# In a four-layer conditional kernel, TensorE computes batch 1's first gate and up ahead of batch 0's first down product

## The reference

```
def _gemma_mlp(x, gate_w, up_w, down_w):
    g = jnp.einsum('bsh,hi->bsi', x, gate_w)
    u = jnp.einsum('bsh,hi->bsi', x, up_w)
    return jnp.einsum('bsi,ih->bsh', jax.nn.gelu(g, approximate=True) * u, down_w)
...
rw = softmax(cond_8);  w, sel = top_k(rw, 2);  w = w / w.sum()
out = sum over the two chosen e of  w[e] * _gemma_mlp(x, skill_gate[e], skill_up[e], skill_down[e])
out = out + _gemma_mlp(x, shared_gate, shared_up, shared_down)
x = x + out
...
up = x @ W_up[best].T + b_up ;  gate = x @ W_gate[best].T + b_gate
x = x + (silu(up) * gate) @ W_down[best].T + b_down
```

## Time and profile before

| | |
|---|---|
| median of 3 runs | 84.12 us (83.91 to 84.49) |
| time of the profiled execution | 85.01 us |
| its span | 83.7 us |
| around the span | 1.3 us |
| TensorE busy | 79.8 us, 95% |
| VectorE, ScalarE, GpSimd busy | 54.7, 37.8, 30.9 us |
| moved by DMA | 20.08 MB, mean 240 GB/s |

### The profile page before, as it was taken

How to read it: one execution, slowest core, us unless ns; L and a number is a source line. 1 busy time by engine, 2 the same in 40 slices (tenths; PEclk the granted TensorE clock), 3 DMA queues, 4 the chain that set the end, 5 groups by cost and what they waited for, 6 DMA issues and landing times.

```text
span 83.7 us, 1689 instructions
## 1 busy us (share of the span) xinstructions
PE 79.8 (95%) x560; PEld 73.8 (88%) x560; DVE 54.7 (65%) x121; ACT 37.8 (45%) x71; POOL 30.9 (37%) x32
## 2 busy tenths in 40 slices
PE   6999999999999999999979999999999999999960
PEld 6968998888888999999978998998998999999960
DVE  1468879865699851489953973973973973844360
ACT  6410895877555930727305434434432132162440
POOL 3020099297666992292900920830830000000000
PEclk9999999999999999999999999999999999999999
DMA  1998000599999998699868999999999954500102
GB/s 17 319 340 350 4 0 0 100 382 343 392 388 395 424 413 327 139 332 357 148 257 263 269 345 344 309 321 398 271 382 375 364 162 78 190 0 0 31 0 67
DMA packets 8792, 20.08 MB, mean 240 GB/s; under 512 B 976, under 2 KB 5200, under 8 KB 8784
## 3 DMA queue, kind: packets, MB, share of 16 engines
q1 hardware_dynamic: 8496, 19.20, 67.5%
q10 hardware_dynamic: 288, 0.79, 2.5%
HBM read 17.88 MB, written 0.52 MB: 220 GB/s over the span
## 4 chain that ended last, share of the span: by engine, by line
PE 86%; DMA 5%; SPq 2%; DVE 2%; issue 0%; DVEq 0%
PE bank L807 17%; PE bank L834 16%; PE bank L848 7%; DMA p<-p 5%; PE bank L863 4%; PE bank L770 4%; PE bank L778 4%; PE bank L786 4%; PE bank L709 4%; PE bank L701 3%; PE bank L820 3%; PE bank L817 3%; PE bank L818 3%; SPq L238 2%; PE bank L794 2%; PE bank L796 2%
## 5 line engine op out<-in xcount | busy, mean ns | idle before, releaser
L353 ACT ACTIVATE gelu<-bank 128x512 f32<-128x512 f32 x24 | 14.2, 595 | 24.0 <-PE bank L820 14.9
L317 POOL TENSOR_TENSOR wide_l<-first_w,wide_h 128x512 fp32r<-128x512 f32 x12 | 15.1, 1277 | 16.8 <-ACT wide_h L378 16.8
L569 DVE SCALAR_TENSOR_TENSOR hid<-gelu,wsel,bank 128x512 f32<-128x512 f32 x16 | 12.0, 747 | 13.1 <-PE bank L820 7.4
L807 PE MATMUL bank<-x_t,second_w 128*128 128x128 f32 x128 | 15.6, 275 | 0.0
L807 PEld LDWEIGHTS bank<-x_t,second_w 128*128 128x128 f32 x128 | 14.9, 192 | 0.0
L308 POOL TENSOR_TENSOR hid_l<-hid,hid_h 128x512 fp32r<-128x512 f32 x8 | 10.2, 1284 | 4.4 <-ACT hid_h L392 4.4
L848 PEld LDWEIGHTS bank<-x_t,w 128*128 128x128 f32 x64 | 8.2, 192 | 0.4
L834 PE MATMUL bank<-hid,second_w 128*128 128x128 f32 x64 | 8.5, 275 | 0.0
L848 PE MATMUL bank<-x_t,w 128*128 128x128 f32 x64 | 8.4, 275 | 0.0
L834 PEld LDWEIGHTS bank<-hid,second_w 128*128 128x128 f32 x64 | 7.9, 192 | 0.1
L567 DVE TENSOR_TENSOR hid<-gelu,bank 128x512 f32<-128x512 f32 x8 | 5.5, 687 | 2.9 <-ACT gelu L353 1.3
(11 more groups left out here) (85 smaller groups left out, 130.3 us busy)
## 6 DMA issues: line engine op xcount, KB each, us to landing
first_w<-in_skill SPq DMA_DIRECT2D x8, 768.0 KB, 6.1
second_w<-in_skill SPq DMA_DIRECT2D x8, 768.0 KB, 6.4
w<-in_layer SPq DMA_DIRECT2D x8, 384.0 KB, 6.5
p<-p SPq DMA_DIRECT2D x24, 64.0 KB, 4.1
rest_sb<-in_rest SPq DMA_DIRECT2D x1, 661.0 KB, 4.4
x_t<-in_x SPq DMA_DIRECT2D x1, 512.0 KB, 5.5
shared_sb<-in_shared ACTq DMA_DIRECT2D x1, 512.0 KB, 5.4
out_x<-out_sb SPq DMA_DIRECT2D x8, 64.0 KB, 4.0
```

The lines of the kernel that those rows point to most:

```text
L317: pool.tensor_tensor(wide_l[:, b % 2, m, :], w[:, m, :], wide_h[:, b % 2, m, :].bitcast(fp32), ALU.subtract).then_inc(wide_low, 1)
L353: act.activation(gelu[:, n, :], ps[:, :], ACT.Gelu_apprx_tanh).then_inc(gelu_ready, 1)
L569: dve.scalar_tensor_tensor(hid[:, n, :], gelu[:, n, :], wsel[:, bass.DynSlice(weight, 1)], u_ps[n][:, :], ALU.mult, ALU.mult).then_inc(hid ...
L807: mm = pe.matmul(ps[:, S * t:S * (t + 1)], w[:, 1 + n, 128 * t:128 * (t + 1)], x2_t[:, columns(b)], start=True, stop=True)
```

## The change

Two calls in TensorE's order change places. No wait, slot, buffer or other engine's order is changed.

```
@@ -907,8 +907,8 @@
                 shared_down(NSH - 3)
                 shared_down(NSH - 2)
                 shared_down(NSH - 1)
+                first_gate_up(1)
                 down(0, 0)
-                first_gate_up(1)
                 batch(1, 1, before_last=False)
```

## The result

The changed kernel takes 86.17 us (median of 4, 85.98 to 87.89) against 84.31 for the kernel before (4 runs). The ratio is 1.023, interval 1.017 to 1.029. The prediction's range ended at 85.1.

A forecast was written before the change was run, and what follows sets the result against it. TensorE was taken as the bound (86% of the chain), with batch 1's swap almost level at `down(1, 0)`. Parts 1 and 2 give 0, part 3 costs 0 to 0.3 us: 84.1 to 84.4, said 84.2, range 83.6 to 85.1.

The forecast's parts named there:

- Part 1: Batch 1's gate and up on TensorE start 0.90 us earlier, hidden values and transpose too; cost 0.
- Part 2: Batch 1's swap on SP, queued behind batch 3's second-expert load, is issued only 0.16 us earlier of 0.90.
- Part 3: `down(0, 0)` ends 1.38 us later, delaying batch 4's first-expert load ahead of the swap; cost 0 to 0.3 us.
- My own sum for the other engines: DMA engines other than the deciding one finish batch 1's swap at 41.9 to 42.4, still ahead of 42.61.
- Rival 1: At `down(1, 0)`: the DMA queue shifts as a whole, swap lands up to 1.38 us later, 85.5; chance 0.15.
- the straggler: DMA engine on the opening backlog until 36.6 sets the swap's landing as before, at 42.6 to 42.9.
- Rivals 2 and 3: At `down(1, 0)`: 2, wait of 0.44 us goes, 83.7, chance 0.15; 3, no wait before or after, 84.1, within 0.58.
- The last sentence of the sum: TensorE is the chain from 42.7 to 76 us, so nothing later gives back a change at `down(1, 0)`.

The follow-up runs named there:

- The kernel with the own tile: Changed order, batch 1's hidden values in a tile of their own so VectorE needn't wait for `down(0, 0)`: 1.018 of before, 85.70 us.
- changed order with five slots: Changed order plus a fifth slot for first experts, so batch 4's first load waits for nothing: 0.998 of before, 84.06 us.
- own tile with the load behind: Changed order, batch 1's hidden values in their own tile and batch 4's first-expert load behind batch 1's swap: 0.993 of before, 84.09 us.
- the run for theory C: Changed order, with the load of batch 4's second expert put behind the swap of batch 2: 1.029 of before, 86.53 us.
- the late-load kernel: Order of before, with batch 4's first-expert load held until batch 1's gate and up are done: 1.017 of before.
- the one with the load behind the swap: Changed order, with batch 4's first-expert load issued behind batch 1's swap: 0.993 of before, 84.17 us.
- the kernel with batch 1's swap first: Old order, with batch 1's swap issued ahead of batch 3's second-expert and batch 4's first-expert loads: 1.015 of before, 85.81 us.
- half the delay: Old order, with batch 4's first-expert load held until batch 1's gate is done: 1.013 of before, 85.57 us.
- The fifth slot: Old order plus a fifth slot for first experts, so batch 4's first load waits for nothing: 1.002 of before, 84.45 us.

## Why the prediction was wrong

**Part 1** failed in its second half. That gate and up could start at once was right: all six products run without a gap. But the hidden values were not made 0.90 us earlier. For batch 1's first expert VectorE waits at L565 for `down(0, 0)`, because that product reads the buffer about to be overwritten (batch 0 isn't in `TURNED`, so the exception in L564 doesn't apply). I read the rows of before, where this wait was always met, and not the code's condition. The new order puts that product last, and the transpose stayed where it was. The kernel with the own tile shows that this cost no time that the runs can tell (1.018 against 1.023).

**Part 2** was right for its own reason (SyncE stands behind `down(0, 1)`). The 0.16 us did not come either; the swap went out 0.59 us behind the second load where it was 0.54.

**Part 3, what the late load does to the landing, is the step that failed.** I argued that one DMA engine sets the landing, that it is on the opening backlog until 36.6, and that a later issue can't show on it; that such an engine ends its backlog before it begins the next load was my assumption, and no run shows it. From the issues and the flights of the L229 and L238 rows: the opening load landed at 36.6 before and 35.9 after, so the backlog was no later, and yet batch 4's load landed at 39.2 in place of 38.5, the next at 41.2 in place of 40.7, the last piece at 43.6 in place of 42.6. Windows of the changed kernel (DMA share and GB/s are the last two numbers), beside the earlier trace rows:

```profile
34.50:35.00 0.50, 0.50 (x7) 0.50 (x7) 0.48 (x1) 0.00 (x0) 0.50 (x1) 1.00 0.00 0
35.00:35.50 0.50, 0.50 (x7) 0.50 (x6) 0.47 (x2) 0.00 (x0) 0.50 (x2) 1.00 0.05 12
...
36.50:37.00 0.50, 0.50 (x6) 0.50 (x6) 0.28 (x2) 0.29 (x1) 0.04 (x1) 1.00 1.01 418
41.00:41.50 0.50, 0.50 (x7) 0.50 (x6) 0.48 (x2) 0.50 (x2) 0.50 (x1) 1.00 1.81 273
```

Next to nothing starts from 34.5 to 35.0, and the full rate comes at 36.5, not 35.5. The DMAs are recorded in packets (8792 on this page), and a window counts a packet, with its whole duration, where it starts; so the 1.81 is mostly the first packets of the next load, which start at 41.35.

One engine does come last, as I read the traces, but it is not behind the opening backlog. The page has a queue of kind `instruction`, q8, with four packets of 16 KB. One of them starts at 39.93 in the kernel before and takes 1.22 us; in the changed kernel it starts at 41.37 and takes 1.11 us (starts and durations of single packets are from the trace's DMA records). The DMA view of the changed kernel for 41.30 to 41.60, 41.60 to 42.46 and 42.46 to 42.95:

```profile
q8 instruction: 1, 0.02, 23.2%
...
DMA packets 8, 0.05 MB, mean 57 GB/s; under 512 B 0, under 2 KB 0, under 8 KB 8
...
DMA packets 37, 0.18 MB, mean 359 GB/s; under 512 B 1, under 2 KB 9, under 8 KB 37
```

The swap moves in packets of 512 bytes (512 of them, from 40.08 to 42.86). All but eight have started by 41.6. None starts from then until the 16 KB packet is at its end (42.48); with it the eight start one after another, from 42.47 to 42.86, as they would on one engine that had them waiting: eight are a sixteenth of one DMA's 128. No record of a packet or of a count names its engine, so this is a reading of the times. `down(1, 0)` waits for 64 counts on one semaphore, 16 from each of the four DMAs (L826). The 63rd came at 42.11, the 64th at 43.61, and the product starts at 43.65. In the kernel before the 61st came at 41.47 and the last three at 42.24, 42.44 and 42.61. The share of 0.07 in the earlier trace rows was, by this reading, this engine, with the swap's packets left over behind its 16 KB.

In eleven of the fourteen traces the last count came 1.1 to 1.5 us after the end of such a packet. In two it had run at 36.1, ahead of the loads' data (changed order with five slots; own tile with the load behind), and there the 48th and the 64th count are 0.6 and 0.3 us apart, not 1.4 to 2.3. In the run for theory C it ran at 38.8, amid the loads, and the last four counts came 0.2 us apart, up to 43.49. So the landing is, by this reading, that of one engine which has a packet of instructions to move besides, and that packet, too, came 1.4 us later in the changed kernel (41.37 against 39.93). TensorE was ready at 42.21 before and 42.00 after. Had the engine kept up with the others (an estimate from the 61st and the 63rd count), the wait would have been nothing before and 0.1 to 0.2 us after. No run moves this packet on purpose, so that the late load costs time only together with it is read from traces and not tested; nor do the runs tell what sets its start.

My own sum for the other engines (41.9 to 42.4) fits the 63rd count at 42.11.

**Rival 1** is what happened, at its mechanism and place. Its price per wait was nearly right: a wait of 1.65 against the 1.78 expected, and a landing later by 1.0 us (1.2 against TensorE's own arrival) where 1.38 was the bound. The time went beyond its 85.5: if most timed runs of the kernel before had no wait, as argued above, the whole wait of 1.65 comes on top of their median and not the shift alone. Its chance of 0.15 was too low: the straggler was read from a landing and a share of 0.07, and not from any row that names an engine. That the swap's landing goes with the loads issued ahead of it is what the late-load kernel and the one with the load behind the swap show, with 1.7% and -0.7%; the size here was most of the shift (1.0 of 1.38 us), not all of it.

**Rivals 2 and 3** did not occur. The first piece of batch 1's swap, 64 KB, landed 2.2 us behind its issue where neither load stood ahead of it (issued at 35.84 in the kernel with batch 1's swap first); behind one load it took 3.9 to 4.0, behind two 4.1 to 5.4. The last sentence of the sum held: what was lost at `down(1, 0)` went on to the end.

## What to carry to other kernels

When a product moves back in an order, list the loads that its end releases, and what stands behind them in the same DMA queue: the price of the move was 768 KB started 1.2 us late ahead of a small transfer that TensorE was about to need. Read the conditions of waits that were always met in the old trace, since a new order can make them the last. Here the load that wasn't urgent did better behind the small transfer that was (0.993 of before and not 1.023), but moving both loads at once only hit the next one (1.21 us of wait at batch 2's swap, 1.015 of before). When several DMAs count on one semaphore, read the last counts before naming the DMA that was late: here, as I read them, it was one engine of 16, with a 16 KB packet of instructions (1.11 us) ahead of its share.

## What the runs showed that was not expected

- The last quarter of the swap's 64 counts took 2.0 us in the changed kernel (from the 48th at 41.58 to the 64th at 43.61), and 1.4 to 2.3 in twelve of the fourteen traces. It goes with the 16 KB packet of queue q8 told above. In nine of the fourteen one of SyncE's own issues near that packet took 1.1 to 1.5 us in place of 0.6 (1.52 at 41.36 in the changed kernel); that these are SyncE's instructions fits this, but no row names their engine.
- From one kernel to the other, with both loads ahead, the last piece landed 8.8 to 9.3 us behind the issue of batch 4's load in six kernels with issues from 33.4 to 34.9, whenever the swap itself was issued (37.5 to 38.4 for the last piece); the seventh, half the delay, had 10.1.
- The fifth slot removed the dependence and won nothing over before in the old order (1.002), though it took 768 KB from the critical stretch.
